# A graph kernel's edge sort: ranks by counts per row and one compare-and-sum each, and 80 more source lists sent in the mean layer

## What is computed

```python
def _L0_gnn_ref(x, W, gamma, beta, edge_weight, edge_row, edge_col):
    agg = segment_sum(edge_weight[:, None] * x[edge_col], edge_row)
    out = concatenate([agg, x], axis=1) @ W.T
    out = (out - mu) * rsqrt(var + EPS) * gamma + beta
    return relu(out)

x = _layernorm(x + _L0_gnn_ref(x, L0_gnn_W, L0_gnn_gamma, L0_gnn_beta, edge_weight, src, dst))
x = _layernorm(x + _L1_gnn_ref(x, edge_index, edge_type_16, ...))   # by relation, two convolutions
x = _layernorm(x + _L2_gnn_ref(x, ..., edge_type_24, 2))            # attention, two hops
x = _layernorm(x + _L3_gnn_ref(x, src, dst, edge_weight, ...))      # interaction layer
```

## Time and profile before

| | us |
|---|---|
| median of 3 runs | 7257.3 (7241.2 to 7273.6) |
| profiled execution, its span | 7237.5 |
| sort phase, until the next phase's first instruction | 0 to 696 |
| mean layer, from the first gather | 708 to about 1717 |
| everything behind it | to 7237 |

### The profile page before, as it was taken

The page is one execution under the profiler, slowest core; times in us unless marked ns, Lnnn a source line. Parts: engine busy times, 40 slices in busy tenths (PEclk is TensorE's granted clock), DMA queues, the critical chain, the costliest instruction groups (busy, mean ns, idle before and its releaser), DMA issues. The chain is left out here.

```text
span 7237.5 us, 161640 instructions
## 1 busy us (share of the span) xinstructions
PE 6315.2 (87%) x35080; PEld 5058.0 (70%) x35081; DVE 5168.2 (71%) x17621; ACT 4246.8 (59%) x14612; POOL 3966.9 (55%) x3682
## 2 busy tenths in 40 slices
PE   5676999997789997889999888887888888899999
PEld 2222788886687776679999766665766666788888
DVE  9887788887655554247777677776666666799998
ACT  0000888885214443138888566665677777677777
POOL 6676777775636666654444444444454444444444
PEclk9555999998879998999999899999898888999999
DMA  1201666666556665557777566665566666444444
GB/s 38 6 2 37 164 189 186 183 196 187 171 153 190 191 191 174 173 177 221 220 222 220 172 200 194 191 193 177 173 199 184 189 188 181 120 125 127 127 127 120
DMA packets 1165457, 1171.57 MB, mean 162 GB/s; under 512 B 308211, under 2 KB 1039755, under 8 KB 1164574
## 3 DMA queue, kind: packets, MB, share of 16 engines
q1 hardware_dynamic: 1007326, 953.22, 43.2%
q0 software_dynamic: 158016, 217.06, 12.7%
HBM read 961.54 MB, written 392.35 MB: 187 GB/s over the span
## 5 line engine op out<-in xcount | busy, mean ns | idle before, releaser
L208 POOL DMA_INDIRECT landing_first<-messages,by_dst_meta x768 | 837.3, 1090 | 723.7 <-PE l1b_ps_b L1481 363.6
L208 POOL DMA_INDIRECT landing_last<-x,by_dst_meta x384 | 438.4, 1142 | 555.9 <-PE l_ps_a L1618 483.1
L1926 POOL DMA_INDIRECT landing_last<-z,by_src_meta x408 | 416.8, 1021 | 578.6 <-PE l2b_ps_g L2225 422.2
L1926 POOL DMA_INDIRECT landing_last<-x,by_src_meta x408 | 419.1, 1027 | 487.8 <-PE l2a_ps_g L2225 283.9
L208 POOL DMA_INDIRECT landing_first<-in_x,by_src_meta x384 | 403.2, 1050 | 182.2 <-issue 89.2
L944 PE MATMUL l_ps_b<-l_w,l_agg_t 128*128 128x256 f32 x1624 | 423.0, 381 | 5.4 <-issue 5.3
L1479 PE MATMUL l1b_ps_b<-root,l1b_x_t 128*128 128x256 f32 x1600 | 426.1, 389 | 0.5
L1479 PE MATMUL l1a_ps_b<-root,l1a_x_t 128*128 128x256 f32 x1584 | 417.8, 386 | 8.3 <-issue 5.7
L941 PE MATMUL l_ps_b<-l_w,l_both 128*128 128x256 f32 x1624 | 422.4, 383 | 0.2 <-issue 0.2
L917 ACT ACT_TABLE_LOAD x1 | 1.3, 1283 | 705.2 <-PEq L117 705.2
L1435 ACT ACTIVATE l1a_x_t<-l1a_ps_x,by_dst_first 128x256 f32<-128x256 f32 x400 | 167.7, 470 | 415.0 <-PE l1a_ps_x L1467 317.5
(11 more groups left out here) (391 smaller groups left out, 20404.9 us busy)
## 6 DMA issues: line engine op xcount, KB each, us to landing
l_both<-in_x_both SPq DMA_DIRECT2D x416, 256.0 KB
l2a_x<-x SPq DMA_DIRECT2D x53, 1216.0 KB
z<-l2a_result SPq DMA_DIRECT2D x400, 152.0 KB
x<-l1b_result SPq DMA_DIRECT2D x392, 152.0 KB
l2b_x<-z SPq DMA_DIRECT2D x53, 1024.0 KB
l1b_x<-h SPq DMA_DIRECT2D x408, 128.0 KB
l1b_res<-x SPq DMA_DIRECT2D x408, 128.0 KB
l2b_res<-x SPq DMA_DIRECT2D x51, 1024.0 KB
```

The costliest lines, as they stand in the source:

```text
L208: pool.indirect_dma_start(gathered[:, slot, 0:D], None, source[0:count, :], bass.IndirectOffsetOnAxis(ap=rows, axis=0), bounds_check=limit ...
L1926: pool.indirect_dma_start(gathered[:, k, :], None, x_in[0:N_NODES, :], bass.IndirectOffsetOnAxis(ap=rows, axis=0), bounds_check=limit, oob ...
```

## The change

In the rank loop the products go. After the histogram loop, whose matmuls now have the identity for ones, `hist[o]` holds the counts of each row. They are copied out; one matmul with ones gives the totals for the chain, and one with `before` plus the seed gives, for each row, the place of its first edge in each bucket, copied to SBUF (`values`). An edge's rank within its row is the number of earlier columns of that row with the same bucket, so one scalar_tensor_tensor over the 392 buckets followed by the earlier columns, with ones for values, gives the whole rank. It reads both tensors from SBUF, grows from 392 to 591 elements, and takes turns over four scratch tiles. The code is unrolled; the small steps for the places are put between columns. `tables.make` moves behind column 127, the chunk kinds behind the ranks, and the drain for `s_rec` ahead of the histogram loop. Pool sends 100 source lists, then only records; the mean layer gets 100 source lists instead of 20, its 300 scatters spread over 192 pairs. Some tiles share memory with dead ones.

```diff
-SOURCES_FIRST = 80
-SOURCES_BEFORE = SOURCES_FIRST + 2 * EC // (RING // 2)
+SOURCES_BEFORE = 100
+SCATTERS_LATER = 2 * EC - SOURCES_BEFORE
...
+                dve.drain().then_inc(s_rec, 1)
+                dve.wait_ge(s_keys, 2)
...
+                def find_rank(column):
+
+                    for o in range(2):
+                        n = column * 2 + o
+                        if n >= JUNKS:
+                            dve.wait_ge(s_rank, n + 1 - JUNKS)
+                        width = WIDTH + column
+                        dve.scalar_tensor_tensor(junk[:, n % JUNKS, 0:width], keys[:, o, 0:width],
+                                                 keys[:, o, width:width + 1], values[:, o, 0:width], ALU.is_equal, ALU.mult,
+                                                 accum_out=rank_f[:, o, column:column + 1]).then_inc(s_rank, 1)
...
+                find_buckets()
+                dve.wait_ge(s_hist, 2 * (EC + RING))
+                for o in range(2):
+                    dve.tensor_copy(row_counts[:, o, :], hist[o][0:EP, :]).then_inc(s_counts, 1)
...
+                    dve.wait_ge(s_total, o + 1)
+                    chain.step(dve.tensor_scalar(b["int"][:], total[o][:], float(P - 1), None, ALU.add))
...
+                for o in range(2):
+                    dve.wait_ge(s_offset, o + 1)
+                    dve.tensor_copy(values[:, o, 0:WIDTH], hist[o][0:EP, :]).then_inc(s_values, 1)
+                dve.wait_ge(s_values, 2)
+                for column in range(EC):
+                    find_rank(column)
+                    quad, part = column // QUAD - 1, column % QUAD
+                    if quad >= 0 and part < 3:
+                        place_part(quad, part)
+                    if column == FIRST_RANKS - 1:
+                        tables.make(dve, c, graphs, chain)
+                        dve.drain().then_inc(s_tab, 1)
...
-                with dve.Fori(0, EC // RING) as g:
-                    for half in range(2):
...
-                            make(column + 1, (k + 1) % RING, s_hot2)
-                            for o in range(2):
-                                a = dve.snap(column + o * (EC + 1))
-                                dve.wait_ge(s_rank, column * 2 + (o + 1))
-                                dve.scalar_tensor_tensor(junk[0:EP, o, :], c.iota[0:EP, :], flat(bucket)[:, bass.ds(a, 1)],
-                                                         rank[o][0:EP, :], ALU.is_equal, ALU.mult,
-                                                         accum_out=rank_f[:, half, o, q:q + 1]).then_inc(s_read, 1)
-                                dve.wait_ge(s_read, column * 2 + (o + 1))
...
-                            pe.matmul(hist[o][:], c.ones_b[0:EP, :], onehot[0:EP, o, k, :], start=False, stop=True,
+                            pe.matmul(hist[o][0:EP, :], c.ident_b[0:EP, 0:EP], onehot[0:EP, o, k, :], start=False, stop=True,
...
+                    pe.matmul(total[o][:], c.ones_b[0:EP, :], row_counts[:, o, :], start=True, stop=True).then_inc(s_total, 1)
...
+                    pe.matmul(hist[o][0:EP, :], c.before[0:EP, 0:EP], row_counts[:, o, :], start=True, stop=False)
+                    pe.wait_ge(s_start, o + 1)
+                    pe.matmul(hist[o][0:EP, :], c.ones[0:1, 0:EP], graphs[o].buckets["seed"][0:1, :], start=False, stop=True)\
+                        .then_inc(s_offset, 1)
...
-                for column in range(SOURCES_FIRST):
+                for column in range(SOURCES_BEFORE):
                     sources.send(column)
...
+                for quad in range(EC // QUAD):
+                    pool.wait_ge(s_placed, 2 * quad + 2)
+                    for q in range(QUAD):
+                        records.send(quad * QUAD + q)
...
-                    for n in range(pair * 6 // 5, (pair + 1) * 6 // 5):
+                    for n in range(pair * SCATTERS_LATER // PAIRS_FIXED, (pair + 1) * SCATTERS_LATER // PAIRS_FIXED):
```

More of the change, by code:

```diff
@@ L457, in sort_edges @@
         s_hot, s_hist, s_start = ph.sem("hot"), ph.sem("hist"), ph.sem("start")
-        s_hot2, s_rank, s_read, s_empty = ph.sem("hot2"), ph.sem("rank"), ph.sem("read"), ph.sem("empty")
+        s_counts, s_total, s_offset, s_values = (ph.sem(n) for n in ("counts", "total", "offset", "values"))
+        s_rank, s_empty = ph.sem("rank"), ph.sem("empty")
         s_int, s_split, s_placed = ph.sem("int"), ph.sem("split"), ph.sem("placed")
@@ L470, in _ @@
             def _(sp):
-                for k, keys in enumerate((src, dst, kind16, kind24)):
-                    sp.dma_start(raw[:, k, :], keys.rearrange("(p c) -> p c", p=EP)).then_inc(s_in, 16)
+                for k, column in enumerate((src, dst, kind16, kind24)):
+                    sp.dma_start(raw[:, k, :], column.rearrange("(p c) -> p c", p=EP)).then_inc(s_in, 16)
                 sp.dma_start(wt[:], weight.rearrange("(p c) -> p c", p=EP)).then_inc(s_in, 16)
@@ new lines, in _ @@
+                chain.step(dve.memset(values[:, :, WIDTH:], 1.0))
+                find_buckets()
+                dve.wait_ge(s_hist, 2 * (EC + RING))
+                for o in range(2):
+                    dve.tensor_copy(row_counts[:, o, :], hist[o][0:EP, :]).then_inc(s_counts, 1)
+                for o in range(2):
+                    b = graphs[o].buckets
+                    dve.wait_ge(s_total, o + 1)
+                    chain.step(dve.tensor_scalar(b["int"][:], total[o][:], float(P - 1), None, ALU.add))
+                    chain.step(dve.tensor_single_scalar(b["int2"][:], b["int"][:], 7, op=ALU.logical_shift_right))
+                    chain.step(dve.tensor_scalar(b["count"][:], b["int2"][:], 1.0, None, ALU.max))
+                    chain.step(dve.tensor_tensor_scan(b["end"][:], c.ones_row[:], b["count"][:], 0.0, ALU.mult, ALU.add))
+                    chain.step(dve.tensor_tensor(b["base"][:], b["end"][:], b["count"][:], ALU.subtract))
+                    dve.tensor_scalar(b["seed"][:], b["base"][:], float(P), None, ALU.mult).then_inc(s_start, 1)
@@ L532, in _ @@
+                for part in range(3):
+                    place_part(EC // QUAD - 1, part)
                 chain.step(dve.tensor_tensor(passed_chunks[:],
@@ L548, in _ @@
-                with dve.Fori(0, EC // RING) as g:
[L549 to L556, removed]
-                    chain.step(dve.tensor_single_scalar(b["int2"][:], b["int"][:], 7, op=ALU.logical_shift_right))
-                    chain.step(dve.tensor_scalar(b["count"][:], b["int2"][:], 1.0, None, ALU.max))
-                    chain.step(dve.tensor_tensor_scan(b["end"][:], c.ones_row[:], b["count"][:], 0.0, ALU.mult, ALU.add))
-                    chain.step(dve.tensor_tensor(b["base"][:], b["end"][:], b["count"][:], ALU.subtract))
-                    chain.step(dve.tensor_scalar(b["seed"][:], b["base"][:], float(P), None, ALU.mult))
```

112 lines of the change are left out of this document (46 added, 66 removed).

## The result

The changed kernel takes 7202.1 us (median; 7192.7 to 7205.3), the kernel before 7258.0 us (7241.2 to 7273.6): a ratio of 0.9925, 95% interval 0.9905 to 0.9946. The profiled execution's span is 7203.6 us against 7237.5.

What follows compares the result with a forecast made beforehand. The prediction took VectorE and Pool as close to each other in the sort phase, with Pool last after the change; -163 us there and +112 in the mean layer gave -51, so 7206 us from the 7257 median, range 7145 to 7245.

Steps and rivals of the forecast that it cites:

- The phase's end, 533: Sort phase: Pool's sends end it at 533 us instead of 696, 163 us gained (118 to 182).
- VectorE, last place at 500: Sort phase: VectorE finishes the last place at 500 us and stays hidden behind Pool by 16 us.
- the small instructions: Rank loop on VectorE: five per four columns' places at 0.16 us each, 41 us (to 95).
- the 4.7 us of exit: Sort phase's end: landing, semaphores and barrier behind the last send take 4.7 us.
- Rival 3: Sort gains less: compare-and-sums keep pitch 0.67 (7238 us), or VectorE slows Pool's sends to 1.8 us (7251); chance 0.23.
- The mean layer, +112: Mean layer: 80 more source lists over 192 pairs take 1049 us instead of 937, +112 us.
- rival 2: Mean layer: Pool's wait for TensorE disappears, so it costs only +61 us, total 7155; chance 0.20.
- Rival 4: Mean layer: TensorE loses its clock, granted clock leaves 1.00; at 0.70 the total is 7328 us; chance 0.05.
- Rival 5: Sort phase: compare-and-sum runs at half rate, 263 us more on VectorE, total 7453 us; chance 0.02.
- The total: Whole kernel: -163 in the sort and +112 in the mean layer give -51 us, 7206 us.

Runs made afterwards that it cites:

- ranks_old_schedule: Kernel before with only the new ranks, keeping Pool's old schedule (180 source lists in the sort, 20 in the mean layer): ratio 0.9972 to the kernel before.
- schedule_old_ranks: Kernel before with only the new schedule (100 source lists first, 100 in the mean layer), old ranks kept: ratio 1.0155 to the kernel before.
- ranks_chained: Changed kernel with a semaphore wait behind every compare-and-sum: ratio 0.9963 to the kernel before, sort ends at 549.4 us.

## Why the prediction was right, point by point

- **The phase's end, 533.** It is 540.9. Pool's first send came at 55.0 us instead of 54.0, the lists had 1.603 for 1.59, records 1.61 for 1.58 (the one send of 4.12 us is half of this), 8 us together; behind the last send it is 3.7 us for 4.7. That Pool is last, which the sum rests on, is shown by ranks_old_schedule and by VectorE's 52 idle us.
- **VectorE, last place at 500.** It is 477.2. Ranks start at 171.3, as said; the pitch is 0.55 and grows to 0.75, as said. Mis-sized were the small instructions: 0.07 to 0.08 us each instead of 0.16, 18 us instead of 41. The 0.38 that the prediction has as their upper end was a mean of 0.59 and 0.17, as schedule_old_ranks shows. A duration was taken where the distance between starts counts, the very thing that I had read off for the compare-and-sums. With the 4.7 us of exit put behind its last instruction, at 488.6, VectorE is hidden by 541-493 = 48 us, not by 16.
- **Rival 3 (0.23).** The chained pitch of 0.67 isn't there; where it was put in (ranks_chained), the end moved by 10 us and not by 48. Its other form, Pool held up by VectorE, is real at 0.11 us a send, and was in the 1.58.
- **The mean layer, +112.** On this chip it is +106: 5.43 us a pair for 5.46, two-pair stretches 10.86 on average for 10.8 to 11. On the quicker kind it is +121: rival 2 (no wait) describes the changed kernel there, 5.24 us for 5.20, but with the old schedule there is no wait there either, 4.61 a pair (ranks_old_schedule), so nothing is gained by it. Rival 2 was priced as if the wait would vanish through the change. Behind the scatters' end a pair takes 3.6 to 4.1 us five times and 4.2 to 4.5 from there, where 4.3 was said.
- **Rival 4 (clock).** The granted clock in the mean layer's scatter stretch is 0.96 instead of 0.99, with TensorE busy 86% of it instead of 93%. The sign named for this case, a clock that leaves 1.00, so did come, but not its price: on the quicker kind the clock is 0.97 and Pool has no waits for TensorE from 900 to 1400 us. I count no time to it.
- **Rival 5 (half rate).** A compare-and-sum with both tensors in SBUF takes 0.63 us at 392 elements, with one in PSUM 0.62: no half rate, against the rule in the Trainium skill's Vector Engine (DVE) Microarchitecture Reference, section 7.
- **The total.** -155.5+106.5 = -49 for -51: the sort gained 7.5 us less than said and the mean layer lost 5.5 less, and that the two misses cancel is luck. From the profiled span of 7237.5 the sum gave 7186, and the profiled execution was 7203.6; from the median 7257 it gave 7206, and the median was 7202. The prediction carried the 19.8 us between span and median over whole, and gave no reason. They aren't time around the span: the changed kernel's profiled execution took 7205.3 us in all, 1.7 over its span. The profiled execution of before was simply a quick one, so that going by the median was right and going by the span was not; this too is luck.

## What to carry to other kernels

Price a move of work from one phase to another by who is last in each, after the other half of the change: the same 80 lists cost at most 21 us in the old loop, were worth 126 us in the new one, and cost 106 or 121 us where they went, by the kind of chip. A mean duration can hide two values: look at what the other engines do beside each. For back-to-back VectorE instructions take the distance between starts, not the duration. Where Pool issues indirect DMAs beside VectorE, keep one of VectorE's two tensors in PSUM; here it was worth 22 us in 200 sends.

## What the runs showed of the hardware that I had not expected

- A VectorE instruction with two SBUF tensors holds an indirect send of Pool until it is over (a send of 4.12 us beside one of 3.74 us), but a stream of 400 of 0.6 to 0.8 us adds only 0.11 us to each send on average.
- It works the other way too: small VectorE steps with one tensor (125x8 int32: L583 and L584 in the kernel before, L568 and L570 in the changed one), started in the last 0.4 to 0.63 us of a send, last until the send is over, up to 0.59 us instead of 0.17. Started earlier in a send, 0.73 to 1.19 us before its end, they take 0.15 to 0.21.
- The copy that fills the keys (784 elements a partition, SBUF to SBUF) ran from 7.46 to 17.75 us beside Pool's memsets, and ended within a microsecond of the last large one. In order of time:

```profile
7.46 10.29 DVE L494 COPY sort_keys<-iota 125x784 f32<-125x784 f32 x1 [5.02 <-PEq L117]
...
15.86 1.29 POOL L647 MEMSET by_dst_meta<- 128x640 int32 x1
...
17.67 0.24 DVE L497 TENSOR_SCALAR sort_bucket_i<-sort_raw 125x200 int32<-125x200 int32 x1
```

- Two kinds of chip: the same kernel takes 6917 or 7250 us. The changed kernel's sort phase is alike in both; the mean layer's pairs take 885 or 937 us with the old schedule (885 with the new ranks) and 1006 or 1043 us with the new one.
